# Projections of the second layer's attention: the rotated products are added by TensorE in PSUM instead of by VectorE in SBUF

## The chip, the cores and the metric

The kernel runs on one core of one Trainium2 chip. The metric is the time of one execution on the device, in microseconds (us), as the median of several runs. Before the change it is 1182.33 us.

## The reference

Two transformer layers work on x of shape (4, 1024, 128). Layer 0 has linear attention and eight experts, of which one is taken for each token. Layer 1 has softmax attention with rotary positions, then sixteen experts and a shared one. The change touches only the projections of layer 1's attention:

```python
h = _layernorm(x) * (1 + ca) + sa
ct_q  = h @ Wd_q_w + Wd_q_b
query = heads(ct_q @ Wu_q_w + Wu_q_b) + heads(_rope(ct_q @ Wq_r_w + Wq_r_b, cos, sin))
ct_kv = h @ Wd_kv_w + Wd_kv_b
key   = heads(ct_kv @ Wu_k_w + Wu_k_b) + heads(_rope(h @ Wk_r_w + Wk_r_b, cos, sin))
value = heads(ct_kv @ Wu_v_w + Wu_v_b)
attn  = softmax(query @ key^T / 12)
```

`_rope(y)` is y * cos plus y with neighbouring features swapped and the sine's sign put in. In the kernel the swap is a second weight matrix with its columns swapped. So query and key are each a sum of three products: the unrotated one, the one times cosine, and the swapped one times sine. Each has its own bias.

## The kernel before, in words

The program is a row of phases: the first layer's attention, its experts, then `phase_project_attention1` (projections and attention of layer 1), the output projection, and the second layer's experts. The projections take the 4096 tokens in eight rounds m = 0..7 of 512 tokens (NM = 8); two rounds are one batch. All data is held transposed, features on the 128 partitions and 512 tokens along the free dimension, in float32. The attention after it needs query and key in bfloat16 with float32 precision, so each is split in three bfloat16 parts: the first part, the rounded remainder, and what is still missing. SyncE stores the parts of a batch to memory once both its rounds are done (`store`), and the attention loads them back by groups of heads.

The order of the work on each engine is written out by hand, and each engine runs its list strictly in that order:

- TensorE (PE), in round m: three matmuls of the query side into three PSUM banks `psR[0]` (L1627, the semaphore is `u_mm`); the transposes of round m+1's normalised tokens (`turn`, L1605); the values (L1634); the down projection of round m+1 (`reduce`, L1611); then three matmuls of the key side into the banks `psR[1]` (L1642, L1644, `k_mm`).
- VectorE (DVE): `rotate` multiplies the second and third bank, with their biases, by cosine and sine (L1431 into `ras`, L1434 into `rbs`). `whole` adds the two in SBUF (L1440), then adds the first bank with its bias (L1444) into `full`. `combine(m + 2)` adds the experts' rows of layer 0 to x and takes the statistics of round m+2 (L1409 to L1424). The remainder of the query side is `full` minus the first part (L1465).
- ScalarE (ACT): in round m `modulated(m+1)` (L1507) and `reduced(m+1)` (L1513) feed the down projection and the next round, `values` (L1518) stores the values, `split` (L1527) rounds `full` to the first part, `second` (L1533) rounds the remainder, and `normalise(m+2)` (L1499) prepares round m+2. `split` and `second` of the key side stand last in the round, ahead of the next round's `modulated`.
- GpSimd (POOL): `rstd` (L1356, L1357), the query side's third part (L1364), the key side's remainder (L1369) and third part (L1371), and four indirect gathers of expert rows for a later round (`gather`, L1348).

The banks of a side are free for the next round once `full` of that side is written (`full_ready`). After the last round DVE negates the first keys (L1472, `nk`), and the attention starts: PE multiplies the difference of keys (L1681, L1685) and the lower half (L1693), ACT takes the positive part (L1574), and DVE reduces (L1479) from 20 such slots, before the long regular part. In all those names "attn" is a large scratch tile in which `ras`, `rbs`, `full`, the remainder and half of the parts lie.

```python
for m in range(NM):
    rotate(m, 0)
    whole(m, 0)
    if m + 2 < NM:
        combine(m + 2)
    ...
    rotate(m, 1)
    whole(m, 1)
```

## Time and profile before

| | us |
|---|---|
| median of three runs (1181.95 to 1185.96) | 1182.33 |
| the profiled execution, its own time | 1185.73 |
| its span in the profile | 1183.5 |
| PE busy | 1049.5 |
| DVE busy | 931.3 |
| ACT busy | 788.5 |
| POOL busy | 325.8 |
| projections: first rotation starts, at | 252.93 |
| projections: DVE starts on the first keys of the attention, at | 343.64 |

The projections are the stretch from 253 to 344 us of the span, under a tenth of it. Busy shares of the whole span say little about them: they are those of the attention (345 to about 970 us) and of the experts.

### The profile page before, as it was taken

The page shows a single profiled execution, that of the slowest core. Times are in us where ns is not written, and L with a number is a line of the kernel's source. Part 1 is how long each engine was busy: PE and PEld are TensorE (multiplying, and loading weights), DVE is VectorE, ACT ScalarE, POOL GpSimd, SP SyncE. Part 2 cuts the span into 40 slices and gives each one's busy share as a digit, 9 for nine tenths or more (in the row PEclk, how much of TensorE's full clock was granted, in tenths as well). Part 3 has the DMA queues.
Part 4 walks back from the last instruction along what each step waited for, and adds up shares of the span by engine and source line. Part 5 has one row for each costly group of instructions (what it writes and reads, how often), then busy time and mean ns, then how long its engine had stood idle before and what let it go on. Part 6 is the DMA issues. An engine that isn't in the chain of part 4 may idle for free. (4 is left out here: it accounts for less than half of the span.)

```text
span 1183.5 us, 23845 instructions
## 1 busy us (share of the span) xinstructions
PE 1049.5 (89%) x9071; PEld 507.1 (43%) x9072; DVE 931.3 (79%) x1464; ACT 788.5 (67%) x1539; POOL 325.8 (28%) x464
## 2 busy tenths in 40 slices
PE   6898599667778999999999999999999999987896
PEld 4787598643331222222222222222222269575554
DVE  7975444368878999999999999999999547755444
ACT  4543433234456999999999999999999955523320
POOL 4632357667630000000000000000000043255354
PEclk9987899888887999999999999999999999999998
DMA  7011266416650101111011110111100003423222
GB/s 239 1 36 37 86 191 180 127 28 176 178 189 3 29 3 29 30 30 29 3 29 30 30 29 4 29 30 30 28 4 2 4 1 137 83 59 83 70 65 71
DMA packets 61160, 72.20 MB, mean 61 GB/s; under 512 B 9941, under 2 KB 40021, under 8 KB 60537
## 3 DMA queue, kind: packets, MB, share of 16 engines
q1 hardware_dynamic: 56184, 60.70, 19.0%
q0 software_dynamic: 4864, 10.00, 3.5%
q8 instruction: 73, 1.20, 0.4%
q14 instruction: 39, 0.31, 0.1%
HBM read 45.41 MB, written 25.18 MB: 60 GB/s over the span
## 5 line engine op out<-in xcount | busy, mean ns | idle before, releaser
L1488 DVE TENSOR_REDUCE mx<-p_psA 128x1 f32<-128x1024 f32 x492 | 563.2, 1217 | 12.6 <-PE p_psA L1656 12.4
L1589 ACT ACTIVATE h<-p_psS 128x512 f32<-128x512 f32 x984 | 527.5, 596 | 38.0 <-PE p_psS L1712 23.3
L1743 PE MATMUL p_acc<-h,p_V 128*32 128x256 f32 x4096 | 326.4, 392 | 14.1 <-ACT attn L1567 13.4
L1712 PE MATMUL p_psS<-Q,K 51*128 51x512 bf16 x984 | 302.7, 384 | 1.4 <-DMA Q<-m_rows 1.4
L1656 PE MATMUL p_psA<-K,Q 48*128 48x512 bf16 x984 | 299.6, 386 | 2.7 <-DVE mx L1488 1.7
L1743 PEld LDWEIGHTS p_acc<-h,p_V 128*32 128x32 f32 x4096 | 83.0, 108 | 208.5 <-ACT h L1589 104.6
L1393 POOL TENSOR_TENSOR mr<-zeros,mx 128x16 f32<-128x16 f32 x32 | 7.2, 224 | 543.7 <-DVE mx L1488 534.4
L1656 PEld LDWEIGHTS p_psA<-K,Q 48*128 48x128 bf16 x984 | 54.5, 94 | 208.1 <-DVE mx L1488 162.3
L1712 PEld LDWEIGHTS p_psS<-Q,K 51*128 51x128 bf16 x984 | 60.0, 93 | 11.9 <-ACT h L1589 9.4
L1074 DVE TENSOR_TENSOR f_h<-f_bank,b 128x512 f32<-128x512 f32 x40 | 27.6, 690 | 40.2 <-PE f_bank L1142 26.6
L1142 PE MATMUL f_bank<-f_xT,f_w 128*128 128x128 f32 x320 | 43.8, 281 | 3.6 <-issue 2.0
L1034 ACT ACTIVATE f_h1T<-f_h 128x512 f32<-128x512 f32 x40 | 25.2, 629 | 32.2 <-DVE f_h L1074 26.9
L2123 POOL DMA_INDIRECT h<-hrows,gidx x32 | 31.4, 982 | 53.3 <-DVE gidx L875 32.8
L1151 PE MATMUL f_mod_ps<-w,f_h1T 128*128 x320 | 42.5, 278 | 0.7 <-DVE f_y L1080 0.7
L991 POOL DMA_INDIRECT h<-hrows,gidx x32 | 30.5, 954 | 44.0 <-DVE gidx L875 21.2
L2134 POOL DMA_INDIRECT h<-result,slot x32 | 32.2, 1006 | 35.7 <-DMA result<-f_shared_kept 15.0
L1142 PEld LDWEIGHTS f_bank<-f_xT,f_w 128*128 128x128 f32 x320 | 39.8, 195 | 4.8 <-issue 2.6
L1151 PEld LDWEIGHTS f_mod_ps<-w,f_h1T 128*128 128x128 f32 x320 | 39.4, 194 | 1.1 <-issue 1.1
L1348 POOL DMA_INDIRECT h<-result,slot x32 | 33.2, 1037 | 17.8 <-issue 8.0
L2182 ACT ACTIVATE f_sg<-f_bank,h 128x128 f32<-128x128 f32 x32 | 11.8, 368 | 38.7 <-PE f_bank L2415 32.4
L1957 ACT ACTIVATE f_shared_sg<-f_bank 128x512 f32<-128x512 f32 x20 | 11.9, 597 | 37.7 <-PE f_bank L1942 31.6
L1942 PE MATMUL f_bank<-hT_l,wsg 128*128 128x512 f32 x64 | 33.2, 601 | 4.0 <-DVE f_m L1970 2.7
(367 smaller groups left out, 1542.6 us busy)
## 6 DMA issues: line engine op xcount, KB each, us to landing
f_w<-in_w SPq DMA_DIRECT2D x40, 256.0 KB
Q<-q_rows SPq DMA_DIRECT2D x32, 192.0 KB, 4.2
K<-k_rows SPq DMA_DIRECT2D x32, 192.0 KB, 4.4
result<-f_shared_kept SPq DMA_DIRECT2D x11, 256.0 KB
result<-f_y SPq DMA_DIRECT2D x10, 256.0 KB
hrows<-h SPq DMA_DIRECT2D x4, 516.0 KB, 7.6
x<-in_x SPq DMA_DIRECT2D x4, 512.0 KB, 5.6
w<-in_w SPq DMA_DIRECT2D x1, 2048.0 KB
```

Source lines behind the costliest of these rows:

```text
L991: pool.indirect_dma_start(out=row_tile(k), out_offset=None, in_=M.hrows0[:, :], in_offset=bass.IndirectOffsetOnAxis(ap=M.gidx[:, k:k + 1], ...
L1142: mm = pe.matmul(ps1[j % 2][:, c * P:(c + 1) * P], w1[j % RING][:, c * P:(c + 1) * P], xT[j // GT % 2][:, j % GT, :], start=True, stop=True)
L1151: mm = pe.matmul(psY[j % 2][:, 0:P], h1T[j % RING][:, c, :], M.w20[:, bass.ds(expert[j], 1), c, :], start=(c == 0), stop=(c == FC0 - 1))
L1348: pool.indirect_dma_start(out=M.h[:, i, :], out_offset=None, in_=M.result0[:, :], in_offset=bass.IndirectOffsetOnAxis(ap=M.slot[:, i:i + 1 ...
L1488: dve.tensor_reduce(mx[v % 2][:, h, qt:qt + 1], psA[t][:], AX.X, ALU.max).then_inc(a_max, 1)
L1589: act.activation(pt[s % 2][:, head_at(s, j), :], psS[k % 3][:], ACT.Exp, scale=INV_SCALE).then_inc(s_out, 1)
L1656: mm = pe.matmul(psA[t][:, c * 512:(c + 1) * 512], Q[g % NBUF][rows, pair, q0:q0 + P], K[g % NBUF][rows, pair, c * 512:(c + 1) * 512], sta ...
L1712: pe.matmul(psS[k % 3][:], K[g % NBUF][rows, h // 2, kc * P:(kc + 1) * P], Q[g % NBUF][rows, h // 2, half * 512:(half + 1) * 512], start=T ...
L1743: mm = pe.matmul(acc[VW * h:VW * (h + 1), cols], V[:, v0 + h * (HD + 1):v0 + h * (HD + 1) + VW], pt[s % 2][:, h, cols], start=(kc == 0 and ...
L1942: pe.matmul(self.bank_g(k)[:], M.wsg1[:, f * P:(f + 1) * P], tok, start=True, stop=True).then_inc(self.g_mm, 1)
L2123: pool.indirect_dma_start(out=row_tile(k, 0, P + 1), out_offset=None, in_=hrows[:, :], in_offset=bass.IndirectOffsetOnAxis(ap=M.gidx[:, k: ...
L2134: pool.indirect_dma_start(out=M.h[:, i, :], out_offset=None, in_=M.result1[:, :], in_offset=bass.IndirectOffsetOnAxis(ap=M.slot[:, i:i + 1 ...
```

## The change

The two rotated products are no longer added in SBUF. PE adds them to the unrotated product, which stays in its bank: after `rotate(m, qk)` two matmuls with the identity as stationary operand (`add_rotated`) put `ras` and `rbs` on top of `psR[qk][0]`. ACT takes the first part from that bank with the bias, and DVE takes the remainder from the same bank, bias and first part in one instruction (`remainder`), for the key side too, which was POOL's before. `full` and `whole` are gone. A bank is free once the remainder was taken (`rest1`). The key side's additions of round m stand on PE in round m+1, behind the query side's three matmuls; its remainder stands on DVE behind the next `rotate(m + 1, 0)`.

```diff
--- before.py
+++ after.py
@@ -1241,7 +1241,8 @@
                                                            n.sem("ct_ready"), n.sem("u_mm"))
         k_mm, v_mm, v_out, bias_mm = n.sem("k_mm"), n.sem("v_mm"), n.sem("v_out"), n.sem("bias_mm")
         bv_ready = n.sem("bv_ready")
-        full_ready, part1, rest1, part2, part3 = ([n.sem(f"{x}{q}") for q in "qk"] for x in ("full_ready", "part1_", "rest1_", "part2_", "part3_"))
+        rotated, sum_mm, part1, rest1, part2, part3 = ([n.sem(f"{x}{q}") for q in "qk"] for x in (
+            "rotated_", "sum_mm_", "part1_", "rest1_", "part2_", "part3_"))
         qk_stored = M.qk_stored
         ones, nmr, bvs = n.sb("ones", [MROWS, L], BF16), n.sb("nmr", [P, NT]), n.sb("bvs", [P, P])
         late = [M.attn[:, u, :] for u in range(BORROWED, 2 * NGRP)]
@@ -1249,7 +1250,7 @@
             M.attn[:, BORROWED + 4:BORROWED + 6, :].rearrange("p c (t e) -> p (c t) e", e=P)
         xn = [late[6 + i].rearrange("p (t e) -> p t e", e=P) for i in range(2)]
         hT, ctT, ras, rbs = late[8:10], late[10:12], late[12:14], late[14:16]
-        full, rest = M.attn[:, BORROWED + 16:BORROWED + 18, :], M.attn[:, BORROWED + 18:BORROWED + 20, :]
+        rest = M.attn[:, BORROWED + 18:BORROWED + 20, :]
         parts = [[n.sb(f"part{i}", [P, 2, L], BF16)[:] for i in range(3)],
                  [M.attn[:, BORROWED + u:BORROWED + u + 2, :].rearrange("p c t -> p (c t)").bitcast(BF16).rearrange("p (k t) -> p k t", k=2)
                   for u in (20, 22, 24)]]
@@ -1362,11 +1363,7 @@
                     pool.wait_ge(rest1[0], m + 1)
                     pool.wait_ge(part2[0], m + 1)
                     pool.tensor_tensor(parts[m // 2 % 2][2][:, 0, j], rest[:, 0, :], parts[m // 2 % 2][1][:, 0, j], ALU.subtract).then_inc(part3[0], 1)
-                    pool.wait_ge(full_ready[1], m + 1)
-                    pool.wait_ge(part1[1], m + 1)
-                    if m >= 1:
-                        pool.wait_ge(part3[1], m)
-                    pool.tensor_tensor(rest[:, 1, :], full[:, 1, :], parts[m // 2 % 2][0][:, 1, j], ALU.subtract).then_inc(rest1[1], 1)
+                    pool.wait_ge(rest1[1], m + 1)
                     pool.wait_ge(part2[1], m + 1)
                     pool.tensor_tensor(parts[m // 2 % 2][2][:, 1, j], rest[:, 1, :], parts[m // 2 % 2][1][:, 1, j], ALU.subtract).then_inc(part3[1], 1)
 
@@ -1429,20 +1426,18 @@
                     bu, j = 1 + 3 * qk, slice((m % 2) * 512, (m % 2) * 512 + 512)
                     dve.wait_ge((u_mm, k_mm)[qk], m + 1)
                     dve.scalar_tensor_tensor(out=ras[qk], in0=a, scalar=M.bcol1[:, bu + 1:bu + 2], in1=rope[:, 0, j],
-                                             op0=ALU.add, op1=ALU.mult).then_inc(dve_step, 1)
-                    link.n += 1
-                    link(dve.scalar_tensor_tensor(out=rbs[qk], in0=s, scalar=M.bcol1[:, bu + 2:bu + 3], in1=rope[:, 1, j],
-                                                  op0=ALU.add, op1=ALU.mult))
-
-                def whole(m, qk):
-
-                    u, bu = psR[qk][0], 1 + 3 * qk
-                    link(dve.tensor_tensor(ras[qk], ras[qk], rbs[qk], ALU.add))
+                                             op0=ALU.add, op1=ALU.mult).then_inc(rotated[qk], 1)
+                    dve.scalar_tensor_tensor(out=rbs[qk], in0=s, scalar=M.bcol1[:, bu + 2:bu + 3], in1=rope[:, 1, j],
+                                             op0=ALU.add, op1=ALU.mult).then_inc(rotated[qk], 1)
+
+                def remainder(m, qk):
+
+                    u, bu, j = psR[qk][0], 1 + 3 * qk, slice((m % 2) * 512, (m % 2) * 512 + 512)
+                    dve.wait_ge(part1[qk], m + 1)
                     if m >= 1:
-                        dve.wait_ge(rest1[qk], m)
-                        dve.wait_ge(part1[qk], m)
-                    dve.scalar_tensor_tensor(out=full[:, qk, :], in0=u, scalar=M.bcol1[:, bu:bu + 1], in1=ras[qk],
-                                             op0=ALU.add, op1=ALU.add).then_inc(full_ready[qk], 1)
+                        dve.wait_ge(part3[qk], m)
+                    dve.scalar_tensor_tensor(out=rest[:, qk, :], in0=u, scalar=M.bcol1[:, bu:bu + 1], in1=parts[m // 2 % 2][0][:, qk, j],
+                                             op0=ALU.add, op1=ALU.subtract).then_inc(rest1[qk], 1)
 
                 dve.memset(V[:, NT * VROW:NT * VROW + VW], 0.0)
                 dve.memset(vout[:, :, :, HD:HD + 1], 1.0)
@@ -1454,17 +1449,14 @@
                 combine(1)
                 dve.wait_ge(ld, 16)
                 for m in range(NM):
-                    j = slice((m % 2) * 512, (m % 2) * 512 + 512)
                     rotate(m, 0)
-                    whole(m, 0)
+                    if m >= 1:
+                        remainder(m - 1, 1)
                     if m + 2 < NM:
                         combine(m + 2)
-                    dve.wait_ge(part1[0], m + 1)
-                    if m >= 1:
-                        dve.wait_ge(part3[0], m)
-                    dve.tensor_tensor(rest[:, 0, :], full[:, 0, :], parts[m // 2 % 2][0][:, 0, j], ALU.subtract).then_inc(rest1[0], 1)
+                    remainder(m, 0)
                     rotate(m, 1)
-                    whole(m, 1)
+                remainder(NM - 1, 1)
 
                 dve.wait_ge(group_in[0], GROUP_IN)
                 for r in range(2):
@@ -1521,10 +1513,11 @@
                 def split(m, qk):
 
                     j = slice((m % 2) * 512, (m % 2) * 512 + 512)
-                    act.wait_ge(full_ready[qk], m + 1)
+                    act.wait_ge(sum_mm[qk], m + 1)
                     if m % 2 == 0 and m >= 4:
                         act.wait_ge(qk_stored[qk][m // 2 % 2], 16 * STORES[qk] * (m // 4))
-                    act.activation(parts[m // 2 % 2][0][:, qk, j], full[:, qk, :], ACT.Copy).then_inc(part1[qk], 1)
+                    act.activation(parts[m // 2 % 2][0][:, qk, j], psR[qk][0], ACT.Identity,
+                                   bias=M.bcol1[:, 1 + 3 * qk:2 + 3 * qk]).then_inc(part1[qk], 1)
 
                 def second(m, qk):
 
@@ -1618,14 +1611,22 @@
                 keep_clock(pe, M, psC, 12)
                 reduce(0)
                 keep_clock(pe, M, psC, 10)
+                def add_rotated(m, qk):
+
+                    pe.wait_ge(rotated[qk], 2 * (m + 1))
+                    pe.matmul(psR[qk][0], M.ident[:], ras[qk], start=False, stop=False)
+                    pe.matmul(psR[qk][0], M.ident[:], rbs[qk], start=False, stop=True).then_inc(sum_mm[qk], 1)
+
                 for m in range(NM):
                     ct, h = ctT[m % 2], hT[m % 2]
                     pe.wait_ge(ct_ready, m + 1)
                     if m >= 1:
-                        pe.wait_ge(full_ready[0], m)
+                        pe.wait_ge(rest1[0], m)
                     for k in range(3):
-                        mm = pe.matmul(psR[0][k], M.wuq1[:, k * P:(k + 1) * P], ct, start=True, stop=True)
+                        mm = pe.matmul(psR[0][k], M.wuq1[:, k * P:(k + 1) * P], ct, start=True, stop=(k > 0))
                     mm.then_inc(u_mm, 1)
+                    if m >= 1:
+                        add_rotated(m - 1, 1)
                     if m + 1 < NM:
                         turn(m + 1)
                     if m >= 1:
@@ -1635,14 +1636,16 @@
                     mm.then_inc(v_mm, 1)
                     if m + 1 < NM:
                         reduce(m + 1)
+                    add_rotated(m, 0)
                     if m >= 1:
-                        pe.wait_ge(full_ready[1], m)
+                        pe.wait_ge(rest1[1], m)
                     else:
                         pe.wait_ge(bv_ready, 2)
-                    pe.matmul(psR[1][0], M.wukv1[:, 0:P], ct, start=True, stop=True)
+                    pe.matmul(psR[1][0], M.wukv1[:, 0:P], ct, start=True, stop=False)
                     for k in range(2):
                         mm = pe.matmul(psR[1][1 + k], M.wkr1[:, k * P:(k + 1) * P], h, start=True, stop=True)
                     mm.then_inc(k_mm, 1)
+                add_rotated(NM - 1, 1)
 
                 def a_part(s, t, c):
 
@@ -1672,12 +1675,12 @@
                             pe.wait_ge(r_ready, fast_before(i))
                         elif i == 0:
                             pe.wait_ge(group_in[0], GROUP_IN)
-                            pe.wait_ge(full_ready[0], NM)
+                            pe.wait_ge(rest1[0], NM)
                         elif i == 1:
                             pe.wait_ge(ct_ready, NM)
                             pe.wait_ge(v_out, NM)
                         elif i == 2:
-                            pe.wait_ge(full_ready[1], NM)
+                            pe.wait_ge(rest1[1], NM)
                         pe.matmul(upper[FAST_SLOT[i]], q, high, start=True, stop=False)
                         return
                     if i < 2:
```

On PE, one whole round in the middle of the projections. In the names, `wuq` are the query side's matmuls, `ident,attn` of 128x128 `turn`, `wukv,attn` the values, `attn,wd` `reduce`, and `attn,wukv` with `attn,wkr` the key side. Before:

```order
L1627 MATMUL p_psA<-attn,wuq 128x512 x2
L1627 MATMUL p_acc<-attn,wuq 128x512
L1605 MATMUL p_psA<-ident,attn 128x128 x4
L1634 MATMUL p_psA<-wukv,attn 128x128 x4
L1611 MATMUL p_psA<-attn,wd 128x512
L1642 MATMUL p_psS<-attn,wukv 128x512
L1644 MATMUL p_psS<-attn,wkr 128x512 x2
```

After:

```order
L1626 MATMUL p_psA<-attn,wuq 128x512 x2
L1626 MATMUL p_acc<-attn,wuq 128x512
L1617 MATMUL p_psS<-attn,ident 128x512
L1618 MATMUL p_psS<-attn,ident 128x512
L1598 MATMUL p_psA<-ident,attn 128x128 x4
L1635 MATMUL p_psA<-wukv,attn 128x128 x4
L1604 MATMUL p_psA<-attn,wd 128x512
L1617 MATMUL p_psA<-attn,ident 128x512
L1618 MATMUL p_psA<-attn,ident 128x512
L1644 MATMUL p_psS<-attn,wukv 128x512
L1646 MATMUL p_psS<-attn,wkr 128x512 x2
```

Four matmuls of 512 columns have come in: two for the previous round's key side (bank in `psS`) ahead of `turn`, two for the query side (bank in `psA`) ahead of the key side's own matmuls.

On DVE, the end of the last round up to the first instruction of the attention (`h<-K`, the negated keys). Before:

```order
L1465 TENSOR_TENSOR attn<-attn 128x512
L1431 SCALAR_TENSOR_TENSOR attn<-p_psS,bcol,attn 128x512
L1434 SCALAR_TENSOR_TENSOR attn<-p_psS,bcol,attn 128x512
L1440 TENSOR_TENSOR attn<-attn 128x512
L1444 SCALAR_TENSOR_TENSOR attn<-p_psS,bcol,attn 128x512
L1472 TENSOR_SCALAR h<-K 48x1024 x2
```

After:

```order
L1439 SCALAR_TENSOR_TENSOR attn<-p_psS,bcol,attn 128x512
L1439 SCALAR_TENSOR_TENSOR attn<-p_psA,bcol,attn 128x512
L1428 SCALAR_TENSOR_TENSOR attn<-p_psS,bcol,attn 128x512
L1430 SCALAR_TENSOR_TENSOR attn<-p_psS,bcol,attn 128x512
L1439 SCALAR_TENSOR_TENSOR attn<-p_psS,bcol,attn 128x512
L1464 TENSOR_SCALAR h<-K 48x1024 x2
```

Three remainders (L1439) stand in the last round: round 6's key side, then round 7's query side, and round 7's key side, which is now the last thing ahead of the attention.

## Rows read from the trace of the kernel before

**Rows 1.** Windows: all rounds, the last round's end, two stretches at the low clock.

```profile
core 0: us, PE busy (x) PEld busy (x) DVE busy (x) ACT busy (x) POOL busy (x), PEclk, DMA share, GB/s
252.93:335.67 82.74, 62.58 (x186) 32.21 (x185) 71.42 (x160) 38.07 (x71) 49.46 (x49) 0.88 0.53 158
335.67:343.64 7.97, 3.66 (x14) 1.56 (x12) 7.13 (x11) 3.00 (x5) 3.47 (x3) 0.90 0.04 15
266.00:269.00 3.00, 1.77 (x2) 0.83 (x3) 2.93 (x7) 1.67 (x3) 2.25 (x2) 0.50 0.00 0
280.00:283.00 3.00, 3.00 (x5) 1.28 (x6) 2.79 (x13) 1.53 (x3) 2.52 (x3) 0.61 0.75 280
```

**Rows 2.** Groups by shape, DVE, 252.9 to 343.7: busy, mean ns | idle before.

```profile
L1440 DVE TENSOR_TENSOR attn<-attn 128x512 f32<-128x512 f32 x16 | 13.9, 866 | 0.5
L1444 DVE SCALAR_TENSOR_TENSOR attn<-p_psA,bcol,attn 128x512 f32<-128x512 f32 x8 | 6.0, 751 | 0.3
L1434 DVE SCALAR_TENSOR_TENSOR attn<-p_psS,bcol,attn 128x512 f32<-128x512 f32 x8 | 5.9, 742 | 0.0
L1465 DVE TENSOR_TENSOR attn<-attn 128x512 f32<-128x512 f32 x4 | 2.8, 693 | 3.1 <-ACT attn L1527 3.1
```

**Rows 3.** Timeline, PE, one round at full clock: start, us, engine, line [idle before].

```profile
289.25 0.66 PE L1605 MATMUL p_psA<-ident,attn 128*128 128x128 f32 x4 [1.39 <-ACT attn L1499]
289.75 1.06 PE L1634 MATMUL p_psA<-wukv,attn 128*128 128x128 f32 x8
292.69 1.13 PE L1611 MATMUL p_psA<-attn,wd 128*128 128x512 f32 x2 [1.89 <-ACT attn L1507]
293.65 1.02 PE L1642 MATMUL p_psS<-attn,wukv 128*128 128x512 f32 x2
294.51 1.88 PE L1644 MATMUL p_psS<-attn,wkr 128*128 128x512 f32 x4
296.23 1.88 PE L1627 MATMUL p_psA<-attn,wuq 128*128 128x512 f32 x4
```

**Rows 4.** Timeline, ACT, the same round.

```profile
291.34 0.63 ACT L1533 ACTIVATE attn<-attn 128x512 bf16<-128x512 f32 x1 [1.62 <-POOL attn L1369]
291.88 0.76 ACT L1507 ACTIVATE attn<-p_psA,modcol 128x512 f32<-128x512 f32 x1
293.86 0.69 ACT L1513 ACTIVATE attn<-p_psA,bcol 128x512 f32<-128x512 f32 x1 [0.73 <-PE p_psA L1611]
```

**Rows 5.** Timeline, PE, the same place in round 1, at the low clock.

```profile
267.23 2.07 PE L1611 MATMUL p_psA<-attn,wd 128*128 128x512 f32 x2 [1.55 <-ACT attn L1507]
269.10 1.67 PE L1642 MATMUL p_psS<-attn,wukv 128*128 128x512 f32 x2
```

**Rows 6.** Timeline, POOL (gather of one round, first and last of four) and DVE (its wait).

```profile
293.43 1.28 POOL L1348 DMA_INDIRECT h<-result,slot  x1 [0.17 <-issue]
297.61 0.94 POOL L1348 DMA_INDIRECT h<-result,slot  x1 [0.30 <-issue]
303.75 2.04 DVE L1409 SCALAR_TENSOR_TENSOR attn<-h,gate,mod 128x128 f32<-128x128 f32 x4 [1.41 <-DMA h<-result,slot]
308.55 0.69 DVE L1465 TENSOR_TENSOR attn<-attn,p_part 128x512 f32<-128x512 f32 x1
```

**Rows 7.** Timeline, PE and DVE: the first round.

```profile
254.12 1.12 PE L1611 MATMUL p_psA<-attn,wd 128*128 128x512 f32 x2
252.93 0.75 DVE L1431 SCALAR_TENSOR_TENSOR attn<-p_psA,bcol,attn 128x512 f32<-128x512 f32 x1 [5.86 <-PE p_acc L1627]
```

**Rows 8.** Timeline, DVE and ACT: where the attention starts.

```profile
343.64 0.86 DVE L1472 TENSOR_SCALAR h<-K 48x1024 bf16<-48x1024 bf16 x2
346.97 0.69 DVE L1479 CUSTOM_DVE_ANT_0 h<-p_psA,h 128x512 f32<-128x512 f32 x1 [2.47 <-PE p_psS L1693]
345.70 0.63 ACT L1533 ACTIVATE attn<-attn 128x512 bf16<-128x512 f32 x1 [1.32 <-POOL attn L1369]
346.24 1.06 ACT L1574 ACTIVATE h<-p_psA 128x512 f32<-128x512 f32 x2
```

## The prediction

> **What bounds the kernel now.** I read the page's busy shares first, then windows over the projections, then the groups by shape there, and last the timelines of single rounds. The whole span doesn't matter: only the stretch from the first rotation (252.93 us) to the first instruction of the attention on DVE (343.64 us) is touched, 90.7 us in all. The seven rounds up to the start of round 7 take 82.74 us, 11.82 us each; DVE is busy for 71.42 us of them, PE for 62.58, POOL for 49.46, ACT for 38.07 [rows 1]. The last round takes another 7.97 us, with DVE at 7.13. So DVE is what sets the rounds now, and PE has slack: it waits for ACT twice in a round, 1.39 and 1.89 us [rows 3]. Those two waits come from the strict order on ACT: its `modulated` stands behind the rounding of the key side's remainder, which waits for POOL [rows 4]. The PE clock is at its upper level, 2.4 GHz, in most of the stretch and at 1.2 GHz (0.50) for all of 266 to 269 us, after PE had little to do [rows 1].
>
> **What leaves.** On DVE, the two additions in SBUF (0.87 us each, 16 in all [rows 2]) and the query side's remainder as a separate step (0.69); the addition with the bank (0.75) turns into the remainder with the bank, of the same shape, so 0.75 stays. The sum of what leaves is 2 x 0.87 + 0.69 = 2.4 us a round, 19 us over eight rounds. On POOL the key side's remainder leaves. Both are real, and if DVE still set the pace they would be the gain. ACT's first part now reads PSUM with a bias: the nearest row is L1513, 0.69 us [rows 4], between 0.63 (the same engine from SBUF) and 0.76 (PSUM with scale and bias) in the same rows. I take 0.69.
>
> **What comes in.** Four float32 matmuls of 512 columns on PE in each round. The trace has no row of them, but their shape is that of L1642: two passes, and the next instruction starts 0.86 us after it (293.65 to 294.51 [rows 3]). At the low clock the same costs 1.51 (269.10, whose pair ends at 270.77 by its modelled end, with 0.16 of drain in it [rows 5]). I take 0.86, since the round will be the densest that PE has here; so 1.72 us for a pair, 3.44 us a round. PE's own work at full clock was 0.50 (`turn`), 0.9 (values), 0.96 (`reduce`), 2.58 (key side) and 2.58 (query side) [rows 3], together 7.5 us; now it is 11.0.
>
> **The chain of one round.** More than the 11.0 counts, because the added matmuls also stand in the middle of the chain that already made PE wait. Let E be the moment when PE has issued the query side's matmuls of round m. Then: previous key side's additions 1.72; to ACT 0.21 (293.65 to 293.86 [rows 3, 4]); first part 0.69; to DVE 0.05; remainder 0.75; to ACT 0.05; its rounding, 0.54 until the next one starts (291.34 to 291.88 [rows 4]); `modulated` 0.76; to PE 0.05. So PE starts `reduce` at E + 4.82. `turn` and the values lie inside (1.72 + 0.5 + 0.9 = 3.1), and PE waits 1.7 us. Then `reduce` 0.96, the query side's additions 1.72, the key side's matmuls 2.58, the next query side's 2.58: the next E is 12.66 us after this one. Before, a round was 11.82 on average. **PE is now the pace.**
>
> Is anything later than this? DVE: two rotations until E + 1.6, idle until the key's remainder (2.67 to 3.42), then `combine`, 4.8 us (303.75 to 308.55 [rows 6]), until 8.2, the query side's remainder at 8.5 to 9.2, needed by PE at E + 10.1: 0.9 us of slack, and its saved 2.4 us are idle time. POOL: the key side's third part, then four gathers (5.1 us from the first to the end of the last, and 5.2 more until DVE has the rows [rows 6]): they land at about E + 15.8, wanted at E + 16.1. If that cover of 0.3 is gone, the 0.9 on DVE covers the next. The waits for stores are two batches back.
>
> **The sum.** In round 0 nothing is saved: PE starts `reduce` at 254.12 [rows 7], then 0.96 + 1.72 + 2.58 + 2.58 gives E1 = 261.96. Six rounds of 12.66 lead to E7 = 337.92, and DVE starts the last round's rotation at 338.13: 2.5 us later than the 335.67 of now. Then the tail. The last round has no `turn` and no `reduce`: additions 1.72, values 0.9, additions 1.72, key side 2.58, to DVE 0.21, rotations 0.66 + 0.74, to PE 0.05, additions 1.72, to ACT 0.21, first part 0.69, to DVE 0.05, remainder 0.67: 11.92 us, against 7.97. The negated keys start at 349.84 instead of 343.64: **6.2 us later**, 2.5 from the rounds and 3.7 net from the tail (3.95 less the 0.21 by which E7 lies ahead of the rotation). One thing comes back. Now ACT is held until 346.24 by the key side's last rounding, which waits for POOL, and DVE's first reduction starts 3.33 us after the negated keys [rows 8]. After the change that rounding runs directly behind the last remainder, so the first reduction could start some 1.9 us after them (0.46 to PE, 0.63 for a matmul, 0.6 for ACT and the handovers): 1.4 us less, of which PE's own pace over the next slots may keep some. I take 1.2. The stores of the last batch start about 4 us later than now, less than the attention does, so nothing new waits for them. Net: **+5.0 us**.
>
> Against the profiled execution (1185.73 us, 0.3% above the median) that is 1190.7; on the median, 1182.33 + 5.0 = **1187.3 us**. 0.5%, about what a measurement of this kernel can tell from no change, is 5.9 us: the forecast lies just inside. The bounds: with 0.63 for the first part and a full 1.4 back, 0.06 x 7 + 0.2 = 0.6 less; if each of the five handovers in the chain costs 0.1 more, 0.5 a round, 3.5 more. With errors of 0.25 us a round for what I read off modelled ends, the case spans +2 to +8.
>
> **Rivals.**
> (a) *The clock falls again.* It was at 1.2 GHz for 266 to 269 us and near it for 280 to 283 (0.61) [rows 1], each time after PE's waits; here PE still waits 1.7 us in a round, and twice in the last one (1.6 and 2.3 us). At the low clock `reduce` and the next matmul took 2.07 and 1.67 instead of 1.13 and 1.02 [rows 3, 5]: 1.6 us more; with the key side's four passes, 2 to 2.5 a stretch. Before, these lie beside DVE's work; after, all are on the path. Three such stretches would add 3 x 2 = 6: 1193.3 us. For it: PE's chain has no slack left. Against it: PE works 11.0 of 12.66 us, where it worked 76% of the time. The page "TensorE: Matmul & The Clock Gate" of the Trainium skill, in its part on oscillation, says the gate closes when PE idles long between bursts, and opens under sustained work; by it the denser round should keep the upper clock, which is how I lean.
> (b) *The additions take one pass, not two.* The matrix is an identity, and the transposes with it cost 0.50 for four of 128 columns against 0.9 for the values [rows 3]. Then 0.86 falls away from each of 2 pairs in six rounds and three times in the tail, 10.3 + 2.6: 5.0 - 12.9 = -7.9, 1174.4 us, faster. PE's work would be 9.2 and DVE's about 9.0 (six instructions of 0.7 and `combine` 4.8), so nothing else holds it much. Against it: these are ordinary matmuls like L1642, and transposes are an instruction of their own. It decides the sign if a pair takes under 1.1 us.
> (c) *The wait for `reduce` is hidden.* If PE never waited, a round would be 11.0 us, and the result 5.0 - 6 x 1.7 = -5.2, 1177.1 us, within the half per cent. The written order on ACT speaks against it. A milder form, a gain at the start of the attention that cancels the loss, would end near 1183.
> (d) *The change is not in effect.* The order of the instructions shows the matmuls in and the additions out, so this gets nothing.
>
> The Trainium skill's "SBUF — State Buffer", in "Who interferes with whom", says that a DVE instruction with two SBUF inputs contends with a POOL instruction that reads SBUF. The trace agrees: L1440 has a mean of 866 ns, and the alike L1465 one of 693 [rows 2]. By that rule the removal is worth a little more than the bare 0.69 us each, on an engine that will have slack; it moves no number above.
>
> **How the numbers follow.** The forecast's case has 0.67 (of it 0.41 within half a per cent, 0.26 above it), (a) 0.18, (b) 0.06, (c) 0.09, of which 0.02 faster than half a per cent. Slower is 0.26 + 0.18 = 0.44; the same 0.41 + 0.07 = 0.48; faster 0.08. The range leaves out (b), most of (c) and the upper part of (a): 1181.5 to 1194.5.
>
> **What would show it.** Right: DVE's rotations of the query side 12.4 to 12.9 us apart from round 1 on; DVE idle for about 2.5 us a round, ended by PE or by ACT's first part; PE's longest wait in a round ahead of `reduce`, for ACT; a pair of additions in 1.72 us; the negated keys near 350. Wrong: rounds of 11.8 or less, pairs under 1.1 us, or a granted clock well under 0.95 over the rounds, which would make it (a).

## The result, and the profile after

| | before | after |
|---|---|---|
| median of 19 runs of each, side by side (us) | 1183.68 | 1187.7 |
| ratio, with its 95% interval | | 1.0035 [1.0021, 1.005] |
| the profiled execution, its own time | 1185.73 | 1187.42 |
| its span | 1183.5 | 1185.6 |
| first rotation to the negated keys | 90.71 | 96.78 |
| first rotation to the first reduction of the attention | 94.04 | 98.42 |

The kernel is slower by 0.35% of 1183.7, 4.1 us (2.5 to 5.9). The spans of the two profiled executions differ by 2.1 us only, because the phases around differ from execution to execution: here the first rotation stood at 255.85 us instead of 252.93, before any added matmul ran. So from here on each kernel's stretch is counted from its own first rotation. The stretch up to the first reduction is 4.38 us longer, which agrees with the measured difference.

The windows of the changed kernel over the same two stretches as [rows 1]:

```profile
core 0: us, PE busy (x) PEld busy (x) DVE busy (x) ACT busy (x) POOL busy (x), PEclk, DMA share, GB/s
255.85:340.86 85.01, 75.64 (x235) 38.13 (x235) 54.17 (x138) 39.99 (x71) 41.88 (x44) 1.00 0.54 155
340.86:352.63 11.77, 9.16 (x28) 3.95 (x26) 4.98 (x7) 3.80 (x6) 2.31 (x2) 1.00 0.27 99
```

DVE's busy time in seven rounds fell from 71.42 to 54.17 us, and the rounds still grew from 82.74 to 85.01. PE went from 62.58 to 75.64, and its granted clock from 0.88 to 1.00: it stayed at 2.4 GHz throughout. The last round grew from 7.97 to 11.77 us.

One round on PE, in the changed kernel's timeline (start, us, engine, line), to be read against [rows 3]:

```profile
277.65 1.02 PE L1617 MATMUL p_psS<-attn,ident 128*128 128x512 f32 x2
278.51 1.02 PE L1618 MATMUL p_psS<-attn,ident 128*128 128x512 f32 x2
279.37 0.60 PE L1598 MATMUL p_psA<-ident,attn 128*128 128x128 f32 x4
279.80 1.06 PE L1635 MATMUL p_psA<-wukv,attn 128*128 128x128 f32 x8
282.42 1.13 PE L1604 MATMUL p_psA<-attn,wd 128*128 128x512 f32 x2 [1.56 <-ACT attn L1499]
283.38 1.02 PE L1617 MATMUL p_psA<-attn,ident 128*128 128x512 f32 x2
284.24 1.02 PE L1618 MATMUL p_psA<-attn,ident 128*128 128x512 f32 x2
285.10 1.02 PE L1644 MATMUL p_psS<-attn,wukv 128*128 128x512 f32 x2
285.96 1.88 PE L1646 MATMUL p_psS<-attn,wkr 128*128 128x512 f32 x4
287.67 1.88 PE L1626 MATMUL p_psA<-attn,wuq 128*128 128x512 f32 x4
289.39 1.02 PE L1626 MATMUL p_acc<-attn,wuq 128*128 128x512 f32 x2
290.25 1.02 PE L1617 MATMUL p_psS<-attn,ident 128*128 128x512 f32 x2
```

A pair of additions takes 1.72 us (277.65 to 279.37). The only wait is the one ahead of `reduce`, 1.56 us. From one key side's additions to the next it is 12.60 us. The same stretch on ACT shows what PE waits for, in the order in which the program has it: the key side's first part, its rounding once DVE has the remainder, then `modulated`:

```profile
279.57 0.69 ACT L1519 ACTIVATE p_part<-p_psS,bcol 128x512 bf16<-128x512 f32 x1 [0.84 <-PE p_psS L1618]
281.07 0.63 ACT L1526 ACTIVATE p_part<-attn 128x512 bf16<-128x512 f32 x1 [0.82 <-DVE attn L1439]
281.61 0.76 ACT L1499 ACTIVATE attn<-p_psA,modcol 128x512 f32<-128x512 f32 x1
```

And the tail on DVE (to be read against [rows 8]): the last rotations, a wait of 2.79 us for the additions and the first part, the last remainder, the negated keys, and the first reduction 1.64 us after these, where it was 3.33 before.

```profile
340.86 0.75 DVE L1428 SCALAR_TENSOR_TENSOR attn<-p_psA,bcol,attn 128x512 f32<-128x512 f32 x1 [1.17 <-PE p_acc L1626]
...
347.76 0.75 DVE L1428 SCALAR_TENSOR_TENSOR attn<-p_psS,bcol,attn 128x512 f32<-128x512 f32 x1 [1.10 <-PE p_psS L1646]
348.43 0.74 DVE L1430 SCALAR_TENSOR_TENSOR attn<-p_psS,bcol,attn 128x512 f32<-128x512 f32 x1
351.96 0.75 DVE L1439 SCALAR_TENSOR_TENSOR attn<-p_psS,bcol,attn 128x512 f32<-128x512 f32 x1 [2.79 <-ACT attn L1519]
352.63 0.86 DVE L1464 TENSOR_SCALAR h<-K 48x1024 bf16<-48x1024 bf16 x2
354.27 0.69 DVE L1471 CUSTOM_DVE_ANT_0 h<-p_psA,h 128x512 f32<-128x512 f32 x1 [0.78 <-PE p_psA L1696]
```

### The profile page after: what moved, and what is told of

The parts are those of the page before. It is cut to its first block and busy times, and to the rows that moved or that the text cites. A ratio compares the mean times of both kernels' runs of the same rounds, so it can differ in the third digit from the quotient of the medians.

```text
span 1185.6 us, 23934 instructions
## 1 busy us (share of the span) xinstructions
PE 1063.1 (90%) x9135; PEld 512.3 (43%) x9136; DVE 913.4 (77%) x1440; ACT 790.6 (67%) x1539; POOL 313.5 (26%) x456
## 5 line engine op out<-in xcount | busy, mean ns | idle before, releaser
L1746 PE MATMUL p_acc<-h,p_V 128*32 128x256 f32 x4096 | 326.8, 393 | 14.1 <-ACT attn L1560 13.4
L1034 ACT ACTIVATE f_h1T<-f_h 128x512 f32<-128x512 f32 x40 | 25.1, 629 | 30.8 <-DVE f_h L1074 30.8
L1491 ACT ACTIVATE attn<-x,p_nmr,rstd 128x128 f32<-128x128 f32 x32 | 13.2, 481 | 40.9 <-POOL p_nmr L1358 40.8
L1960 ACT ACTIVATE f_shared_sg<-f_bank 128x512 f32<-128x512 f32 x20 | 11.9, 597 | 37.7 <-PE f_bank L1945 37.7
```

The source lines that it names most:

```text
L1746: mm = pe.matmul(acc[VW * h:VW * (h + 1), cols], V[:, v0 + h * (HD + 1):v0 + h * (HD + 1) + VW], pt[s % 2][:, h, cols], start=(kc == 0 and ...
```

## The experiments

This table has every kernel's stretch, from start times in the DVE timeline: the seven rounds (from one query side's first rotation to the next), the last such rotation to the negated keys, from there to the first reduction, and the sum. Beside it stands the ratio to the kernel before, over 4 executions in experiment 1, 6 in 4 and 10, 10 or 12 in the others and 19 of the change, while the stretch is of one execution only.

| kernel | rounds 0 to 6, us | sum | to keys | to reduction | in all | ratio [interval] |
|---|---|---|---|---|---|---|
| before | 10.87 11.56 12.80 11.11 12.72 13.68 10.00 | 82.74 | 7.97 | 3.33 | 94.04 | 1 |
| the change | 9.40 12.60 12.60 12.60 12.60 12.60 12.61 | 85.01 | 11.77 | 1.64 | 98.42 | 1.0035 [1.0021, 1.005] |
| 1: third addition | 10.45 14.32 14.31 14.32 14.31 14.32 14.32 | 96.35 | 14.35 | 1.64 | 112.34 | 1.0147 [1.0123, 1.0171] |
| 2: change, ACT's order | 9.23 11.52 11.65 11.55 13.82 11.51 11.16 | 80.44 | 11.77 | 1.65 | 93.86 | 0.9999 [0.9979, 1.0018] |
| 3: one addition | 9.68 11.39 11.58 11.62 12.84 11.32 10.88 | 79.31 | 12.11 | 1.87 | 93.29 | 0.9979 [0.9958, 1.0001] |
| 4: before, ACT's order | 10.88 11.03 11.05 12.08 13.13 11.80 8.22 | 78.19 | 7.96 | 3.34 | 89.49 | 0.9945 [0.9923, 0.9966] |
| 5: query side only | 9.49 13.41 13.41 13.40 13.41 13.40 13.41 | 89.93 | 8.89 | 3.34 | 102.16 | 1.0016 [0.9996, 1.0036] |
| 6: 5 and ACT's order | 9.50 10.28 13.23 10.91 13.28 10.91 9.76 | 77.87 | 8.90 | 3.33 | 90.10 | 0.9967 [0.995, 0.9984] |
| 7: two additions, moves | 9.23 11.51 11.51 11.51 12.33 11.50 11.16 | 78.75 | 8.23 | 4.93 | 91.91 | 0.9978 [0.9964, 0.9992] |
| 8: one addition, moves | 9.61 11.73 13.10 11.63 11.35 11.31 9.44 | 78.17 | 8.77 | 4.08 | 91.02 | 0.9978 [0.9962, 0.9993] |
| 9: 5, PE kept busy | 9.49 11.73 12.62 11.92 13.49 11.72 11.72 | 82.69 | 8.89 | 3.33 | 94.91 | 1.0013 [0.9994, 1.0031] |
| 10: 6, remainder and gathers moved | 9.49 11.02 10.12 10.12 11.36 10.53 9.76 | 72.40 | 8.90 | 2.89 | 84.19 | 0.9903 [0.9886, 0.992] |
| 11: negated keys first | 9.23 12.60 12.60 12.60 12.60 12.60 12.60 | 84.83 | 8.23 | 4.93 | 97.99 | 1.004 [1.0021, 1.0059] |
| 12: the moves alone | 10.87 12.99 12.99 12.98 11.75 11.90 10.04 | 83.52 | 8.11 | 2.89 | 94.52 | 0.9982 [0.9963, 1] |

The theory going in: the added matmuls lie on the path that sets a round, and the chain through ACT makes PE wait besides. The rivals: the additions lie in slack and only the handovers cost; or DVE still sets the rounds.

**1. The suspected cost half as large again.** Each pair of additions got a third matmul, to `after`:

```diff
                     pe.matmul(psR[qk][0], M.ident[:], ras[qk], start=False, stop=False)
+                    pe.matmul(psR[qk][0], M.ident[:], ras[qk], start=False, stop=False)
                     pe.matmul(psR[qk][0], M.ident[:], rbs[qk], start=False, stop=True).then_inc(sum_mm[qk], 1)
```

> The changed kernel with a third identity matmul in every pair (the cosine product is put on top once more, so query and key are other numbers). Theory (TensorE's added matmuls are on the path that sets a round): 0.86 us more per group: 0.86 in round 0, 1.72 in each of six rounds (12.60 to 14.3 us from rotation to rotation), 2.6 in the tail, 13.8 us more than the change, ratio to the kernel before about 1.015. Rival (the additions lie in TensorE's slack and the loss comes from the waits between engines): rounds stay at 12.6, no more than 2.6 us more from the tail.

The ratio is 1.0147, rounds 14.32 us, the tail 14.35: in all 13.92 us more than the change, of 13.8 expected. Both groups of each of the 8 tiles cost their 0.86 us in the end, since 16 x 0.86 = 13.8. In this kernel's timeline the three stand 0.86 us apart:

```profile
280.17 1.02 PE L1617 MATMUL p_psS<-attn,ident 128*128 128x512 f32 x2
281.03 1.02 PE L1618 MATMUL p_psS<-attn,ident 128*128 128x512 f32 x2
281.89 1.02 PE L1619 MATMUL p_psS<-attn,ident 128*128 128x512 f32 x2
```

The slack rival falls.

**2. The order on ACT, in the changed kernel.**

```diff
-                    if m + 1 < NM:
-                        modulated(m + 1)
+                    if m == 0:
+                        modulated(1)
                     values(m)
...
                     split(m, 1)
+                    if m + 2 < NM:
+                        modulated(m + 2)
                     second(m, 1)
```

> The changed kernel, with ScalarE's modulated(m + 2) moved between the key side's first part and the rounding of its remainder. Theory (a round is the chain additions, first part, remainder, rounding, modulated, reduce): the reduce matmul starts 3.3 us after the query side's matmuls instead of 4.8, rounds of 11.2 us where nothing else holds them; the gathers of expert rows land too late in rounds 2 to 5 then and may keep these at about 12.2. In all 4 to 8.5 us less than the change: ratio to the kernel before 0.996 to 1.000. Rival (PE's own work or the DVE sets a round): 12.6 us as now, ratio 1.0035.

0.9999, 4.56 us less in the stretch: at the mild end of what was expected. Rounds of 11.5 us where 11.2 was expected (PE is busy for 11.27 us of the first of them), and one of 13.82, in which DVE waited 2.38 us for gathered rows (its timeline):

```profile
311.50 1.14 DVE L1406 SCALAR_TENSOR_TENSOR attn<-h,gate,mod 128x128 f32<-128x128 f32 x4 [2.38 <-DMA h<-result,slot]
```

So PE's wait ahead of `reduce` was on the path. Taking it out gave about 1.1 us a round, and then PE has next to no wait left.

**3. One addition by each engine.** DVE adds `ras` and `rbs` in SBUF, PE puts the sum on the bank:

```diff
-                    pe.wait_ge(rotated[qk], 2 * (m + 1))
-                    pe.matmul(psR[qk][0], M.ident[:], ras[qk], start=False, stop=False)
-                    pe.matmul(psR[qk][0], M.ident[:], rbs[qk], start=False, stop=True).then_inc(sum_mm[qk], 1)
+                    pe.wait_ge(rotated[qk], m + 1)
+                    pe.matmul(psR[qk][0], M.ident[:], ras[qk], start=False, stop=True).then_inc(sum_mm[qk], 1)
...
+                def both(m, qk):
+                    dve.wait_ge(dve_step, link.n)
+                    dve.tensor_tensor(ras[qk], ras[qk], rbs[qk], ALU.add).then_inc(rotated[qk], 1)
```

(`both(m, 0)` is called ahead of `combine`, `both(m, 1)` behind `rotate(m, 1)`.)

> Half the change: VectorE adds the two rotated products in SBUF as before, TensorE puts their sum on the bank with one matmul instead of two; the rest as in the change. Theory (PE's matmuls are on the path, VectorE has some 2.5 us of idle time in a round): 0.86 in round 0, up to 1.7 in each of six rounds (10.9 to 11.5 us), about 1.8 in the tail: 8 to 12 us less than the change, ratio 0.994 to 0.998. Rival (the handovers between engines cost, not the matmuls, and an addition on VectorE in the chain costs as much as one on TensorE): within 2 us of the change, ratio 1.002 to 1.005.

0.9979, 5.13 us less than the change in the stretch, against 8 to 12 expected. Rounds came to 11.3 to 11.6, with one of 12.84 and the last of 10.88, where 10.9 to 11.5 was expected. The tail did not shorten (12.11 instead of 11.77): there the DVE addition stands in the chain too. The direction is the theory's, the size is not.

**4. The order on ACT, in the kernel before.** The same edit as in 2, to `before`.

> The kernel before, with the same move of ScalarE's modulated(m + 2). Theory (VectorE and GpSimd set its rounds, TensorE's wait ahead of reduce is beside them): at most VectorE's idle time ahead of the key side's rotation, some 1 to 3 us in all, ratio 0.997 to 1.000. Rival (the same chain through ScalarE sets its rounds too): 1.5 us in each of six rounds, ratio about 0.992.

A miss. The ratio is 0.9945, 6.5 us, and 4.55 us in the stretch; 1 to 3 were expected. One line of the groups tells it. The wait of DVE ahead of the key side's rotation, 4.9 us for PE in the kernel before, is 0.2 here:

```profile
L1431 DVE SCALAR_TENSOR_TENSOR attn<-p_psS,bcol,attn 128x512 f32<-128x512 f32 x7 | 5.2, 745 | 0.2 <-PE p_psS L1646 0.2
```

The kernel before was held by the same chain through ACT in a part of its rounds. Its 4.9 us are four waits, of 0.44, 1.65, 2.13 and 0.65 us. The first three fall in rounds in which PE's clock was down (granted clock 0.71, 0.87 and 0.75). One of them, in the timelines of PE and DVE:

```profile
279.89 1.38 PE L1611 MATMUL p_psA<-attn,wd 128*128 128x512 f32 x2 [1.89 <-ACT attn L1507]
281.06 1.91 PE L1642 MATMUL p_psS<-attn,wukv 128*128 128x512 f32 x2
285.33 0.75 DVE L1431 SCALAR_TENSOR_TENSOR attn<-p_psS,bcol,attn 128x512 f32<-128x512 f32 x1 [1.65 <-PE p_psS L1644]
```

L1642 takes 1.70 us here until the next instruction, and 0.86 in the round of [rows 3], where PE waits as long for ACT (1.39 and 1.89 us), the clock is 1.00 and DVE does not wait at all. So in those rounds it was the wait for ACT and the slow matmuls behind it together. In kernel 4 the clock falls too (0.85 to 0.87 in four rounds), but PE starts `reduce` 2.7 us after the round's first rotation (278.73 to 281.41) instead of 4.5 (275.36 to 279.89), and DVE waits no more than 0.2. This one edit beats both kernels.

**5. Half the change.** Only the query side's products are added by PE; the key side has its sum, `full` and POOL's remainder as before.

```diff
                     rotate(m, 0)
-                    if m >= 1:
-                        remainder(m - 1, 1)
...
                     rotate(m, 1)
-                remainder(NM - 1, 1)
+                    key_sum(m)
...
-                    if m >= 1:
-                        add_rotated(m - 1, 1)
...
-                add_rotated(NM - 1, 1)
```

(`key_sum` is the two instructions of `whole`.)

> Half the change: only the query side's rotated products are added by TensorE; the key side is as in the kernel before (sum in SBUF by VectorE, remainder by GpSimd). Theory (the key side's pair of additions and its remainder stand in the chain ahead of reduce, and its last pair in the tail): rounds of about 11.8 us instead of 12.60, the last rotation to the negated keys about 9.5 instead of 11.8 us, the start of the attention 1.7 us worse again: about 5.5 us less than the change, ratio 0.998 to 1.000. Rival (any addition on TensorE costs the same wherever it stands): half of the change's loss comes back, ratio about 1.0015 to 1.002.

The tail came close to what was said (8.89 for 9.5, and 3.34), the rounds did not: 13.4 instead of 11.8. The profile shows why. PE waits 2.38 us ahead of `reduce`, not 1.56, and then its clock falls in every round:

```profile
322.75 1.13 PE L1620 MATMUL p_psA<-attn,wd 128*128 128x512 f32 x2 [2.38 <-ACT attn L1512]
323.71 1.85 PE L1633 MATMUL p_psA<-attn,ident 128*128 128x512 f32 x2
325.35 1.91 PE L1634 MATMUL p_psA<-attn,ident 128*128 128x512 f32 x2
```

The pair takes 3.35 us (323.71 to 327.06, where the key side's first matmul starts) instead of 1.72. Over 78 us the granted clock is 0.87, as the window below shows (the columns are those of [rows 1]). The ratio over twelve executions is 1.0016 though, and this profiled execution, at 1192.55 us, was the longest of them (median 1183.27): the clock can hardly have fallen so in all. The granted clock over each whole execution says the same: 0.958 in this one, the lowest of the twelve, and 0.960 to 0.973 in the others. By the ratio alone the theory (0.998 to 1.000) misses and the rival (1.0015 to 1.002) stands; the medians do not exclude that half of the additions cost half of the loss.

```profile
262.00:340.00 78.00, 63.67 (x176) 31.16 (x176) 53.94 (x122) 35.61 (x65) 44.34 (x46) 0.87 0.54 156
```

**9. The same, with PE kept busy in that wait.**

```diff
+                    if 1 <= m < NM - 1:
+                        pe.wait_ge(full_ready, m)
+                        keep_clock(pe, M, psR[1][0], 28)
                     if m + 1 < NM:
                         reduce(m + 1)
```

> The fifth kernel (query side only by TensorE), and in the wait ahead of reduce, in rounds 1 to 6, 28 small matmuls of ones on a free bank that nobody reads (about 1.6 us of work). Theory (its rounds of 13.4 us hold 2 us that come from the TensorE clock, which falls each time after the wait of 2.4 us): granted clock 1.00 over the rounds, the pair of additions in 1.72 us instead of 3.3, rounds of 11.4 to 11.6 us: 11 to 12 us less than the fifth kernel, ratio about 0.992. Rival (the additions are slow there for another reason, as the bank that VectorE and ScalarE read): rounds stay at 13.4, ratio 1.0016.

The window of this kernel:

```profile
262.00:340.00 78.00, 70.12 (x357) 39.25 (x355) 55.64 (x124) 36.70 (x66) 47.06 (x46) 1.00 0.55 166
```

It is the stretch shown of 5, and its clock is 1.00. In the timeline, behind 28 small matmuls in the wait, the pair is back at 1.71 us (302.70 to 304.41):

```profile
299.98 1.73 PE L170 MATMUL p_psS<-onesb 128*128 128x128 bf16 x28
301.73 1.12 PE L1620 MATMUL p_psA<-attn,wd 128*128 128x512 f32 x2
302.70 1.02 PE L1633 MATMUL p_psA<-attn,ident 128*128 128x512 f32 x2
303.56 1.02 PE L1634 MATMUL p_psA<-attn,ident 128*128 128x512 f32 x2
304.41 1.02 PE L1661 MATMUL p_psS<-attn,wukv 128*128 128x512 f32 x2
```

Four rounds are 11.7 to 11.9 us; two stay at 12.6 and 13.5. The stretch is 7.25 us shorter than in 5. The ratio, 1.0013, is that of 5, not the 0.992 expected, and the clock of its whole executions (0.963 to 0.975) is hardly above that of 5. So what the low clock costs is shown for one execution of kernel 5; that it decides the median of kernel 5 is not shown, and the ratio of kernel 9 speaks against it. I over-read a single profile. The page "TensorE: Matmul & The Clock Gate" of the Trainium skill tells in its part on oscillation of a kernel whose long waits between bursts of matmuls close the gate, and in "A second HAM failure mode: psum-queue depth-cycling" of one in which frequent short ones do. The profile of kernel 5 is like the second (0.87 with a wait of 2.38 us in every round, 1.00 with it filled); that of the changed kernel, with a wait of 1.56 us in every round and 1.00, is not.

**6. Half the change and the order on ACT** (the edits of 5 and 2 together).

> The same, with ScalarE's modulated(m + 2) moved between the key side's first part and the rounding of its remainder. Theory: nothing of TensorE's is left waiting in a round, so VectorE (about 10 us of work) or GpSimd (about 9.9 us of work with the gathers) sets it, 10.2 to 11.2 us; ratio 0.991 to 0.996, at or below the kernel before with that move (0.9945). Rival (TensorE's additions still set the round): 11.8, ratio 0.998 to 1.000.

0.9967, just above the expected range of 0.991 to 0.996. Rounds of 10.3 to 10.9, but two of 13.2. In both POOL had four gathers ahead of `rstd`, PE waited 2.04 and 2.52 us for the `normalise` behind it, and the granted clock of the round was 0.87; in the second DVE also waited 4.29 us for gathered rows. The rival of 11.8 us a round falls; what is left was GpSimd's lateness and the clock after it. But 0.9967 is not below kernel 4 (0.9945): with this one move alone, the additions on PE brought nothing.

**7 and 8. More moves, with two and with one addition by PE.** Beside the edit of 2 (and of 3 in kernel 8), POOL's gathers and DVE's negated keys are moved up:

```diff
+                    if m + 4 < NM:
+                        gather(m + 4)
                     pool.wait_ge(rest1[1], m + 1)
...
-                remainder(NM - 1, 1)
-
                 dve.wait_ge(group_in[0], GROUP_IN)
...
+                remainder(NM - 1, 1)
```

> The changed kernel, both additions by TensorE, with three moves: ScalarE's modulated(m + 2) as in the second experiment, GpSimd's gathers ahead of the key side's third part, and VectorE's negated keys ahead of the last remainder. Theory (in the second experiment the gathers came too late in rounds 2 to 5): rounds of 11.2 us throughout, the first reduction 0.4 us earlier: 8 to 9 us less than the change, ratio 0.995 to 0.997. Rival (the gathers are not what held those rounds): as the second experiment, ratio about 1.000.

> One addition by TensorE, the other by VectorE, as in the third experiment, with the same three moves. Theory: TensorE has 9.3 us of work in a round and VectorE 10.4, so VectorE sets it, 10.6 us: some 6 us less than the third experiment, ratio 0.992 to 0.994. Rival (a handover sets the round, whichever engine adds): 11.2 us as with two additions, ratio about 0.996.

Both 0.9978. With two additions the long round of 13.82 went to 12.33 and the others stay at 11.5, and the ratio is 0.0057 below that of the change, 6.7 us (6.51 in the stretch, 98.42 less 91.91), where 8 to 9 was expected. With one addition the rounds were 11.3 to 11.7 and one 13.10 (granted clock 0.89), not 10.6. So it is the rival, more than the theory, that holds for 8. The rounds are alike, but what ends them is not. In 7 it is PE's own work: it is busy for 11.28 us of a round of 11.51. In 8 PE is busy for 9.56 us of 11.31, and waits for DVE to free the query side's bank, since that remainder (L1445) stands behind `combine`: PE's next query side matmuls, at 317.47, start after 1.63 us of waiting for it.

**10. The version that the experiments point to.** As 6, with the key side's remainder by DVE behind the next rotation, and the gathers of 7:

```diff
                     rotate(m, 0)
+                    if m >= 1:
+                        key_rest(m - 1)
                     if m + 2 < NM:
                         combine(m + 2)
```

(`key_rest` is one subtraction in SBUF; the last one stands behind the negated keys.)

> The sixth kernel (query side only by TensorE, ScalarE's modulated(m + 2) moved), with the key side's remainder taken by VectorE instead of GpSimd, behind the next rotation, and GpSimd's gathers ahead of the key side's third part. Theory (the rounds of 13.2 us in the sixth were waits for gathers that GpSimd issued late, and low clock after them): VectorE has 10.7 us of work in a round and sets it, 10.8 to 11 us throughout, the first reduction about 1 us earlier: 3 us less than the kernel before with the one move, ratio 0.991 to 0.993. Rival (something else makes the long rounds): as the sixth, 0.9967.

0.9903 [0.9886, 0.992], 11.5 us faster than the kernel before and a little better than the 0.991 to 0.993 expected. Rounds of 10.1 to 11.4 (9.5 and 9.8 the first and last), no wait for gathers, a granted clock of 1.00, and PE and DVE are now about equally busy. Which of the two moves did more was not tried. Its window:

```profile
262.00:335.00 73.00, 64.45 (x204) 31.58 (x202) 63.72 (x139) 37.86 (x69) 39.35 (x41) 1.00 0.59 179
```

**11. The negated keys ahead of the last remainder, in the changed kernel.** (The last part of the edit of 7.)

> The changed kernel, with VectorE's negated keys ahead of the last remainder instead of behind it. Theory (the last additions, first part and remainder are a chain of their own that ends in the banks and engines which the first differences need too): the first reduction only 0.2 to 0.5 us earlier than in the change, ratio 1.003. Rival (the tail costs because the negated keys stand behind the last remainder): the first reduction comes 3 us earlier, ratio about 1.001.

The keys come 3.54 us earlier behind the last rotation, and the first reduction only 0.43 behind the first one (97.99 instead of 98.42), of which 0.17 is round 0: 1.004. The tail is the chain of additions, first part and remainder, and not the place of the keys.

**12. Are the additions on PE worth anything?** The moves of 10 in the kernel before, with no addition by PE (`key_rest` behind `rotate(m, 0)`, ahead of `whole(m, 0)`).

> The tenth kernel's moves in the kernel before, with no addition by TensorE: ScalarE's modulated(m + 2) ahead of the rounding, GpSimd's gathers ahead of the key side's third part, the key side's remainder by VectorE behind the next rotation. Theory (TensorE's additions for the query side are worth something once nothing else waits: they take 0.9 us of a sum and no more from VectorE, which sets the rounds): VectorE has 11.5 to 12 us of work in a round with combine, rounds of 11.5, ratio 0.993 to 0.997, 3 to 7 us more than the tenth. Rival (all of the tenth's gain is the moves): ratio 0.989 to 0.991.

0.9982: the rival, all of 10's gain from the moves, falls clearly. It is also worse than the theory said, and worse than 4 with its single move. DVE waits for no other engine in those three rounds of 12.99 us: it is busy for 12.61 of them, where 11.5 to 12 was expected, and for 10.65 to 11.70 in kernel 4. A part is the key side's remainder, 0.69 us, which DVE now has; beyond that, its own instructions got longer. The groups of DVE over three rounds, of this kernel and then of kernel 4, show the four small products of `combine` (x12 for three rounds):

```profile
L1405 DVE SCALAR_TENSOR_TENSOR attn<-h,gate,mod 128x128 f32<-128x128 f32 x12 | 7.9, 718 | 0.0
```

```profile
L1409 DVE SCALAR_TENSOR_TENSOR attn<-h,gate,mod 128x128 f32<-128x128 f32 x12 | 4.7, 448 | 0.0
```

718 ns each instead of 448, and the addition L1436 1084 ns in the mean instead of 840; against that, the addition of `combine` (L1409, L1413 in kernel 4) went from 1250 ns to 690. In the timelines, the four products that take 2.64 us lie over a POOL instruction that reads SBUF. Of the two additions L1436 below, the long one does so too, and beside the short one POOL has only a gather:

```profile
298.25 2.64 DVE L1405 SCALAR_TENSOR_TENSOR attn<-h,gate,mod 128x128 f32<-128x128 f32 x4
```

```profile
299.05 1.16 POOL L1369 TENSOR_TENSOR attn<-attn 128x512 bf16<-128x512 f32 x1
```

```profile
296.87 0.68 DVE L1436 TENSOR_TENSOR attn<-attn 128x512 f32<-128x512 f32 x1
305.62 1.48 DVE L1436 TENSOR_TENSOR attn<-attn 128x512 f32<-128x512 f32 x1
305.41 1.15 POOL L1364 TENSOR_TENSOR attn<-attn 128x512 bf16<-128x512 f32 x1
```

That the overlap is the cause is read from where the instructions lie; no run took it away. And this profiled execution, at 1188.09 us, was the longest of its twelve (median 1182.13), so its rounds may overstate what the median lost.

## Why the prediction was right, and where its reasons were not

- **The sum.** +5.0 us was forecast; measured 4.1 (2.5 to 5.9), and 4.38 in the stretch of the two profiles. The median, 1187.7, stands 0.4 us from the forecast 1187.3, but that is partly luck: the median of the kernel before was 1183.68 in these runs, not 1182.33.
- **What comes in.** "1.72 us for a pair" is what the trace has. The rival of a single pass, and the faster case with it, is out. Its sum also left out the query side's pair of round 0: experiment 1 shows 16 groups, not 15.
- **The chain of one round.** `reduce` at E + 4.82 and a round of 12.66 us were forecast. Measured: 277.65 to 282.42, so 4.77, and 12.60. Experiments 1 and 2 show both halves: 0.86 more in a group makes a round 1.72 longer, and taking the rounding out of the chain makes it 1.1 shorter (1.5 by the sum, but PE's own work then fills 11.3 of 11.5 us).
- **The tail.** 11.92 us from E7, so 11.71 from the rotation, and 11.77 measured. What comes back at the start of the attention was 1.69 us (3.33 less 1.64), of which I had taken 1.2. These 0.5 us are most of the difference between 5.0 and 4.38.
- **The clock.** Rival (a) did not come true: 1.00 over all rounds. In the profile of kernel 5, where the wait is 2.38 us and not 1.56, the clock did fall. What (a) said of the kernel before, that its stretches at the low clock "lie beside DVE's work", was misread: DVE waits 1.65 and 2.13 us behind two of them (experiment 4).
- **The covers.** The cover of 0.3 us for the gathers was gone in one round (DVE waited 1.31 us at 307.55) and the slack behind it took it up: that round is 12.60 like the others. DVE's idle time was put at about 2.5 us a round; it was 4.4 (30.8 us in seven).
- **What was wrong:** the step "DVE is what sets the rounds now". It was read from DVE's busy share of 86%. Experiment 4 took 6.5 us from the kernel before without touching DVE's work. Its rounds were held in turn by DVE, by gathers and by the chain through ACT, with the low clock behind it. That chain I had named in the same paragraph and then treated as slack. The forecast did not hang on it, as only the new chain entered the sum, but the expectation of 4 did.
- **Also open.** Why the profiled execution of kernel 5 stands 9.3 us above the median is shown only in part: its clock over the whole execution was the lowest of the twelve, but where in the others the clock was higher was not profiled.

## What to carry to other kernels

An addition moved from a full engine to one with idle time is not free if it stands in the chain that makes that engine idle: follow one round from its slowest handover back to itself, with the new instruction in it, and compare its length with the old round. Before moving work, look for an instruction that stands behind an unrelated wait in a strict order; here one such move on ScalarE gave 6.5 us. With that move alone the query side's additions on TensorE still brought nothing (0.9967 in kernel 6, 0.9945 in kernel 4). They paid once GpSimd's remainder and gathers had been moved too: kernel 10 is 5 us below kernel 4 and 9 us below kernel 12, which has the same moves without them. A part of those 9 us is the longer instructions of kernel 12 and not the additions; the two were not told apart. With both sides' additions on TensorE no order that was tried came below 0.9978.

## What the runs showed of the hardware

- In two profiles of nearly the same kernel, a PE wait of 1.56 us in each round of 12.6 left the granted clock at 1.00, and one of 2.38 us let it fall to 0.87 over the rounds; 28 small matmuls in the wait kept it at 1.00. The length of the wait alone does not decide it: in the kernel before, with waits of 1.39 and 1.89 us in the round, the clock was 1.00 in the round of [rows 3] and 0.87 in the one before it.
- A float32 matmul with the identity as stationary operand that accumulates on a bank cost the same 0.86 us for 512 columns as those of the key side (L1644), also while DVE read another bank (L1428 at 277.85, beside the additions at 277.65).
- With GpSimd's work moved by a few us, VectorE's instruction times changed without a wait in sight: from 448 to 718 ns for the 128x128 products, and between 0.68 and 1.49 us for the addition L1436. The Trainium skill, "SBUF — State Buffer", "Who interferes with whom", has DVE instructions with two SBUF inputs contend with POOL's reads; the trace agrees (1.48 us over L1364, 0.68 with no such POOL instruction beside it). An order that is better on paper can lose to that, as experiment 12 did.
